# Two transformer layers on one core: every wide product and norm transpose in tiles of 64 rows, values' products in two visits a sample

## The reference

```
mod = silu(c) @ w_mod + b_mod            # shift, scale, gate twice
h = layernorm(x) * (1 + scale) + shift
q, k, v = split(h @ w_qkv + b_qkv)       # 16 heads of 18
# layer 0 only: q and k are layer-normed per head, with a gain
o = softmax(q @ k.T * 18**-0.5) @ v
x = x + gate * (o @ w_proj + b_proj)
h = layernorm(x) * (1 + scale2) + shift2
x = x + gate2 * (gelu(h @ w1 + b1) @ w2 + b2)     # 1152 hidden
```

## Time and profile before

| | |
|---|---|
| time, median of 3 runs | 2496.43 us (2495.59 to 2497.12) |
| profiled execution | 2496.4 us from its first to its last instruction, with nothing outside that span given |
| TensorE matmul busy | 2328.6 us, 93% |
| TensorE weight loads busy | 1975.0 us, 79% |
| VectorE busy | 1899.0 us, 76% |
| ScalarE busy | 1643.7 us, 66% |
| GpSimd busy | 733.8 us, 29% |

### The profile page before, as it was taken

The page is one execution under the profiler, slowest core; times in us unless marked ns, Lnnn a source line. Parts: engine busy times, 40 slices in busy tenths (PEclk is TensorE's granted clock), DMA queues, the critical chain, the costliest instruction groups (busy, mean ns, idle before and its releaser), DMA issues.

```text
span 2496.4 us, 74800 instructions
## 1 busy us (share of the span) xinstructions
PE 2328.6 (93%) x29875; PEld 1975.0 (79%) x29875; DVE 1899.0 (76%) x3456; ACT 1643.7 (66%) x3305; POOL 733.8 (29%) x938
## 2 busy tenths in 40 slices
PE   5658999999999999999899899999999999999988
PEld 3446888888888888888788788888888888888877
DVE  6457888778778888877777788778877887787764
ACT  2356777777777777776666666666666666666653
POOL 2111332333233233323222223233322332233222
PEclk7778999999999999999999999999999999999999
DMA  3777667766765776576666565455555564555431
GB/s 100 143 178 121 113 123 125 123 119 123 130 112 122 127 117 126 122 129 113 131 113 109 133 112 99 100 107 109 103 100 105 104 109 98 108 98 109 90 72 44
DMA packets 259280, 282.07 MB, mean 113 GB/s; under 512 B 25930, under 2 KB 243212, under 8 KB 258936
## 3 DMA queue, kind: packets, MB, share of 16 engines
q1 hardware_dynamic: 243888, 247.40, 53.1%
q10 hardware_dynamic: 15048, 29.89, 5.5%
HBM read 101.86 MB, written 26.73 MB: 52 GB/s over the span
## 4 chain that ended last, share of the span: by engine, by line
PE 66%; DMA 9%; SPq 7%; DVE 6%; issue 4%; POOL 4%; ACT 2%; DVEq 0%; ACTq 0%; POOLq 0%
PE psum L838 17%; PE psum L1082 15%; PE psum L961 8%; PE psum_max L838 6%; SPq L1497 5%; PE psum_exp L937 4%; PE psum L828 4%; PE psum_max L950 4%; DMA attn_k_stack<-attn_qk_hi 4%; PE psum_exp L838 3%; DMA attn_o_and_sums<-attn_o_transposed 3%; DVE attn_maxima L1237 2%; SPq L1447 2%; PE psum_max L866 1%; POOL mlp_ln_split L1439 1%
## 5 line engine op out<-in xcount | busy, mean ns | idle before, releaser
L1237 DVE TENSOR_REDUCE attn_maxima<-psum_max 128x4 f32<-128x1024 f32 x512 | 621.8, 1214 | 202.4 <-PE psum_max L950 201.6
L1102 ACT ACTIVATE attn_probs<-psum_exp 128x1024 f32<-128x1024 f32 x512 | 524.4, 1024 | 166.9 <-PE psum_exp L937 157.7
L1082 PE MATMUL psum<-mlp_w_fc_hi,mlp_hidden_hi 64*128 64x288 f32 (+1 forms) x2250 | 343.6, 293 | 0.5 <-ACT mlp_hidden L1184 0.5
L1082 PE MATMUL psum<-mlp_w_fc_hi,mlp_hidden_lo 64*128 64x288 f32 (+1 forms) x2250 | 343.6, 292 | 0.0
L1082 PE MATMUL psum<-mlp_w_fc_lo,mlp_hidden_hi 64*128 64x288 f32 (+1 forms) x2250 | 341.2, 290 | 0.0
L1410 POOL TENSOR_TENSOR mlp_x<-mlp_x,mlp_gated 128x288 f32<-128x288 f32 x128 | 119.7, 935 | 616.9 <-DVE mlp_gated L1254 616.9
L961 PE MATMUL psum<-attn_probs,attn_v 128*32 128x256 f32 x4096 | 281.5, 393 | 2.1 <-DVE attn_neg_max_lo L1264 1.8
L937 PE MATMUL psum_exp<-attn_q_stack,attn_k_stack 64*128 64x256 f32 x2048 | 245.2, 317 | 21.3 <-DMA attn_q_stack<-attn_neg_max_lo 10.2
L838 PE MATMUL psum_max<-mlp_ln_split,mlp_w_fc_stacked 64*128 64x256 f32 (+1 forms) x3584 | 264.5, 284 | 0.1
L838 PE MATMUL psum<-attn_ln_split,w_qkv_split 128*128 128x256 f32 (+3 forms) x2282 | 251.4, 291 | 12.5 <-ACT attn_qk_squares L1148 5.2
L937 PEld LDWEIGHTS psum_exp<-attn_q_stack,attn_k_stack 64*128 64x128 f32 x2048 | 158.5, 187 | 129.8 <-issue 73.9
(11 more groups left out here) (181 smaller groups left out, 4496.4 us busy)
## 6 DMA issues: line engine op xcount, KB each, us to landing
attn_q_stack<-attn_qk_hi SPq DMA_DIRECT2D x256, 128.0 KB
attn_k_stack<-attn_qk_hi SPq DMA_DIRECT2D x256, 128.0 KB
attn_o_and_sums<-attn_o_transposed SPq DMA_DIRECT2D x256, 128.0 KB, 3.3
mlp_gate_and_gated_bias<-modulation ACTq DMA_DIRECT2D x64, 288.0 KB, 4.9
attn_qk_squares<-qk_rstd SPq DMA_DIRECT2D x32, 512.0 KB
attn_q_stack<-attn_qk_lo SPq DMA_DIRECT2D x128, 128.0 KB
attn_k_stack<-attn_qk_lo SPq DMA_DIRECT2D x128, 128.0 KB
attn_x<-in_x_dram SPq DMA_DIRECT2D x32, 288.0 KB, 6.0
```

What stands on the lines that cost most here:

```text
L1082: mm = q.matmul(to[t], (h_hi, h_hi, h_lo)[kind][r, c, t * P:t * P + P], (w2_hi, w2_lo, w2_hi)[kind][r, c, :], start=(i == 0 and not second ...
L1102: q.activation(probs[r][:], ps_exp[:], ACT.Exp, scale=SCORE_SCALE).then_inc(S["exps"], 1)
L1237: q.tensor_reduce(maxes[g % 2][:, p // QUARTER, :, p % QUARTER, :], ps_max[:].rearrange("p a (t n) -> p a t n", t=TT), AX.X, ALU.max).then ...
```

## The change

- `spaced` goes. q/k, v, projection, fc1 and fc2 are always cut in halves of 64 rows. The last q/k chunk is cut as well: its two token halves are two products of 128 tokens in two banks, in two parts, LAST_FIRST and LAST_SECOND.
- fc1 runs its nine chunks in one loop: the lower rows of one chunk beside the upper rows of the chunk two steps later.
- The norm transposes take 64 tokens each, twelve in place of six, into two banks by token half; ScalarE reads both banks with one instruction.
- The values' products come in two visits a sample, of two groups each, side by side in bank 4 (512 columns), with one copy for both; P_RING goes from 3 to 4.
- The tiles of the modulated norm and of the gated product are shared by attention and MLP, with waits for the other's use.
- The slots are eighths rather than quarters, and nearly all offsets and banks are new. Offsets of TensorE's work are shown, those of the other engines' are left out, as is the bookkeeping of banks and semaphores.

```diff
+VISITS = GROUPS // 2
...
-STACK_RING, V_RING, P_RING, XA_RING, XR_RING = 2, 3, 3, 2, 3
...
-SPAN, STEP = 16, 4
+STACK_RING, V_RING, P_RING, XA_RING, XR_RING = 2, 3, 4, 2, 3
...
+SPAN, STEP = 16, 8
...
-LN_TR, LN_Y, LN_SPLIT = (-46.25, -30.5, {B + 1: -35.25}), (-46.75, -31.25, {B + 1: -35.5}), (-40.25, -30.75)
...
+LN_TR, LN_Y, LN_SPLIT = (-46.625, -31.125, {B + 1: -34.75}), (-47.5, -31.25, {B + 1: -35.125}), (-39.5, -30.25)
...
-LAST_CHUNK_AT = (-34.5, -27.5, {3: -36.0})
-QK_FIRST, QK_SECOND = [(-33.0, -26.0, {B - 1: -31.75}), (-32.75, -16.75)], [(-32.25, -25.0, {B - 1: -31.5}), (-32.25, -16.75, {2: -32.0, B - 1: -31.5})]
...
-V_FIRST, V_SECOND, V_OUT = (-26.0, -17.75, {1: -31.0, B: -17.5}), (-25.5, -17.5, {1: -30.0, 2: -24.0, B + 1: -16.0}), [(-25.0, -17.5, {1: -29.5}), (-24.25, -16.75)]
-VAR_AT, RS_AT = (-28.75, -28.75, {B - 1: -29.0}), (-29.0, -29.0, {0: -31.5})
...
-MAX_AT, MAX_OUT, MAX_TR, NEG_AT, NEG_PLACE = -11.5, -11, [(-4.25, -4.25), (3.75, 5.5, {ALL - 1: 3.0})], [(-4.5, -4.5), (4.25, 5.25)], [(-3.75, -6.0, {0: 0.25}), (5.5, 3.25, {B: 7.0})]
-EXP_AT, EXP_OUT, PV_AT, PV_OUT = 0, 0.25, 5.75, 5.75
...
-XR_AT, GATE_AT, PROJ_FIRST, PROJ_SECOND = (23.75, 21.5, {B - 1: 23.25}), (24.0, 22.5), (26.5, 26.5), (27.0, 28.75)
...
-LAST_FC1_AT, FC1_AT, HIDDEN_AT, H_SPLIT = (49.75, 48.75, {B: 47.75}), 49.75, 49.75, [(49.75, 50.0), (49.75, 50.25), (50.0, 50.25), (50.25, 50.75), (50.5, 50.75)]
+LAST_FIRST, LAST_SECOND = (-34.75, -26.375, {3: -33.75}), (-34.25, -26.25, {3: -33.5})
+QK_FIRST, QK_SECOND = [(-33.625, -25.625, {B - 1: -33.625}), (-32.0, -16.25)], [(-32.75, -24.5, {B - 1: -32.125}), (-31.25, -16.125, {2: -30.625, B - 1: -30.625})]
...
+V_FIRST, V_SECOND, V_OUT = (-27.25, -18.125, {1: -28.625, B: -17.5}), (-26.0, -17.375, {1: -24.75, 2: -23.25, B + 1: -17.625}), [(-25.125, -17.375, {1: -22.875}), (-22.875, -17.0)]
+VAR_AT, RS_AT = (-29.0, -56.625, {B - 1: -28.5}), (-28.5, -34.875, {0: -31.875})
...
+MAX_AT, MAX_OUT, MAX_TR, NEG_AT, NEG_PLACE = -11.5, -11.125, [(-4.25, -4.125), (3.875, 3.75, {ALL - 1: 3.875})], [(-4.0, -3.875), (3.25, 4.125)], [(-0.375, 0.75, {0: 1.125}), (3.125, 4.5, {B: 3.25})]
+EXP_AT, EXP_OUT, PV_AT, PV_OUT = 0, 0.125, 3.75, 3.75
...
+XR_AT, GATE_AT, PROJ_FIRST, PROJ_SECOND = (24.875, 28.0, {B - 1: 20.25}), (21.25, 16.75), (26.0, 28.625), (27.5, 29.75)
...
+TR2, Y2, SPLIT2, SPLIT2_LOW, GATE2_AT = (41.875, 41.125), (41.25, 41.125), (43.625, 43.75, {ALL - 1: 37.25, B: 43.375}), (41.625, 39.0, {ALL - 1: 27.5}), (55.125, 51.5)
+FC1_AT, HIDDEN_AT, H_SPLIT = 49.75, 48.875, [(50.25, 50.0), (50.25, 50.625), (50.25, 50.625), (50.625, 50.625), (50.875, 51.25)]
...
-FC2_AT = [(49.75, 50.0), (51.0, 50.5), (55.75, 55.5), (56.75, 57.25)]
...
+FC2_AT = [(50.125, 50.0), (54.875, 53.25), (56.625, 56.125), (57.625, 57.625)]
...
-TURN_BANKS, LN_REST_BANK, LN2_REST_BANK = ((4, 4), (7, 2)), (3, 7), (7, 7)
-FC1_FIRST, FC1_SECOND, LAST_FC1_BANK = (0, 1, 2, 3), ((5, 4, 0, 1), (6, 4, 0, 1)), (7, 6)
-QK_BANKS, LAST_CHUNK_BANK, VAR_BANK = [((4, 7), (7, 4)), ((5, 6), (6, 5))], (6, 7), 4
-V_BANKS, PROJ_BANKS, FC2_BANKS = ((4, 7), (7, 4)), ((7, 5), (7, 5)), ((5, 6), (5, 6))
-LN_BANK, LN2_BANK = (5, 5), (1, 0)
+TURN_BANKS = ((7, 7), (7, 7))
+FC1_BANKS = ((1, 7, 4, 0, 5, 6, 3, 2, 0), (7, 2, 0, 1, 3, 6, 5, 4, 1))
+QK_BANKS, LAST_CHUNK_BANK, VAR_BANK = [((4, 7), (7, 4)), ((5, 6), (5, 4))], (5, 0), 7
+V_BANKS, PROJ_BANKS, FC2_BANKS = ((4, 7), (7, 6)), ((7, 5), (4, 5)), ((5, 6), (6, 5))
+LN_BANK, LN2_BANK = (2, 5), (0, 2)
...
+FC1_STEPS, FC1_APART = [5, 7, 8, 0, 1, 2, 3, 4, 6], 2
+FC1_BEGUN = [0, 2, 1, 3, 4, 5, 6, 7, 8]
...
+def visit_at(T, off):
+
+    last = VISITS * ALL
+    if T in (LAST_PV, LAST_PV_OUT):
+        return last if (T, off) in ((LAST_PV, PV_AT), (LAST_PV_OUT, PV_OUT)) else None
+    w, r = divmod(T - off, SPAN // VISITS)
+    return int(w) if r == 0 and 0 <= w < last else None
+
+
+def groups_of(w):
+
+    return [s for s in (2 * w - 1, 2 * w) if 0 <= s < GROUPS * ALL]
...
+        y2_ab, y2_c = y_ab, y_c
...
+        gated2 = gated
...
+        LOWER, UPPER = slice(0, HALF_ROWS), slice(HALF_ROWS, P)
...
+        def lower_and_upper(q, low, high, half):
+
+            for i in range(len(WIDE_PAIRS)):
                 done_low = part_matmul(q, low, i, LOWER, i == 0, False)
                 done_high = part_matmul(q, high, i, UPPER, i == 0, False)
...
+            done_low.then_inc(S[half], 1)
+            done_high.then_inc(S[half], 1)
+            halves[half] = halves.get(half, 0) + 2
+
+        def upper_and_lower(q, low, high):
 
             for i in range(len(WIDE_PAIRS)):
-                first, last = not split and i == 0, i == len(WIDE_PAIRS) - 1
-                done_low = part_matmul(q, low, i, UPPER if split else ROWS, first, last)
-                done_high = part_matmul(q, high, i, LOWER if split else ROWS, first, last)
+                last = i == len(WIDE_PAIRS) - 1
+                done_low = part_matmul(q, low, i, UPPER, False, last)
+                done_high = part_matmul(q, high, i, LOWER, False, last)
             return done_low, done_high
...
+        def to_channels(q, banks, src):
+
+            for c in range(3):
+                cols = slice(c * P, c * P + P) if c < 2 else slice(2 * P, XC)
                 for t in range(TT):
-                    mm_ab = q.transpose(ab[:, c * N + t * P:c * N + t * P + P], src[:, t, c * P:c * P + P], ident[:])
-            for t in range(TT):
-                mm_last = q.transpose(last[0:K3, t * P:t * P + P], src[:, t, 2 * P:XC], ident[:])
-            return mm_ab, mm_last
-
-        def ln_modulate(q, g, kind, turned, free, from_banks, to_ab, to_c, done):
+                    for bank, r in zip(banks, (LOWER, UPPER)):
+                        mm = q.transpose(bank[0:cols.stop - cols.start, c * P + t * HALF_ROWS:c * P + t * HALF_ROWS + HALF_ROWS], src[r, t, cols], ident[r, r])
+            return mm
...
+            def last_product(g, t):
+                return (psum[banks["qk", g, 4, t][0]][0:QK_ROWS[4], 0:P], w_attn, slice(4 * P, 4 * P + QK_ROWS[4]), acts, slice(t * P, t * P + P), True, LAST_ROWS)
+
...
+                if (w := visit_at(T, PV_AT)) is not None:
+                    bank = bank_of(("pv", w))
+                    for s in groups_of(w):
+                        g, grp = divmod(s, GROUPS)
+                        if grp == 0:
+                            q.wait_ge(S["v_ready"], TT * (g + 1))
+                        q.wait_ge(S["exps"], PAIRS * g + 2 * grp + 2)
+                        cols = slice(N * (s % 2 == 0), N * (s % 2 == 0) + N)
+                        for t in range(TT):
+                            for i in range(PV_HEADS):
+                                pair = PAIRS * g + 2 * grp + i // HALVES
+                                mm = q.matmul(bank[32 * i:32 * i + VW, cols], v_sb[g % V_RING][:, t, grp * PV_HEADS + i, :, :].rearrange("p r c -> p (r c)"),
+                                              probs[pair % P_RING][:, i % HALVES, t * N:t * N + N], start=(t == 0), stop=(t == TT - 1))
+                        mm.then_inc(S["pv"], 1)
...
+                if (g := due(T, LAST_FIRST)) is not None:
...
+                    bank_of(("qk", g, 4, 0))
+                    bank_of(("qk", g, 4, 1))
+                    lower_and_upper(q, *[last_product(g, t) for t in range(TT)], "last_half")
+                    LAST_HALVES[g] = halves["last_half"]
+                if (g := due(T, LAST_SECOND)) is not None:
+                    q.wait_ge(S["last_half"], LAST_HALVES[g])
+                    low, high = upper_and_lower(q, *[last_product(g, t) for t in range(TT)])
+                    high.then_inc(S["qk_mm"], 1)
...
+                        q.wait_ge(S["qk_half"], QK_HALVES[g, n])
+                        low, high = upper_and_lower(q, *[qk_product(g, c) for c in pair])
...
+                    q.wait_ge(S["v_half"], halves["v_half"])
+                    low, high = upper_and_lower(q, *[v_product(g, t) for t in range(TT)])
...
+                    q.wait_ge(S["proj_half"], halves["proj_half"])
+                    low, high = upper_and_lower(q, *[proj_product(g, t) for t in range(TT)])
...
+                    for k in range(CHUNKS):
+                        low, high = [fc1_product(g, FC1_STEPS[(k + n) % CHUNKS]) for n in (0, FC1_APART)]
+                        low_ends, high_ends = k >= FC1_APART, k + FC1_APART >= CHUNKS
+                        if not low_ends:
+                            bank_of(("fc1", g, FC1_STEPS[k]))
+                        if not high_ends:
+                            bank_of(("fc1", g, FC1_STEPS[k + FC1_APART]))
+                        if low_ends:
+                            q.wait_ge(S["fc1_half"], CHUNKS * g + (2 if k == FC1_APART else k + 1))
+                        for i in range(len(WIDE_PAIRS)):
+                            ends = i == len(WIDE_PAIRS) - 1
+                            done_low = part_matmul(q, low, i, LOWER, i == 0 and not low_ends, ends and low_ends)
```

(16 more changed lines are left out.)

259 lines of the change are left out of this document (101 added, 158 removed).

## The result

The changed kernel takes 2517.59 us (median of four runs, 2515.91 to 2521.16), the kernel before 2496.01 beside it (2494.86 to 2497.12): a ratio of 1.0088, 95% interval [1.0074, 1.0102]. The forecast was 2435, and both the time and its sign are wrong.

What follows compares the result with a forecast made beforehand. TensorE's stream was taken to set the steady pace. Net gains of 0.9 us over 30 layer 0 samples and 1.1 over 31 layer 1 samples sum to 61 us: 2496.4 - 61 = 2435 us, range 2398 to 2475.

Steps and rivals of the forecast that it cites:

- Waits: TensorE's waits for banks and other engines: gain of 0.1 us a sample in layer 0, 0.8 in layer 1 (bounds 0, 1.4).
- the other edits cost nothing here: Shared norm and gate tiles and fourth probabilities buffer: cost 0, covered by VectorE's 200 us idle in each stretch.
- The rival with this mechanism: Waits take the gain as VectorE and ScalarE do the same work in less time: about 2470 us, chance 0.16.
- The prediction's own sign of being wrong: It would be wrong if transposes took 1.3 us or TensorE's list of waits grew past 1 us a sample.
- The rival priced at 2515: Slower: halves' weight loads don't overlap, norm transposes run singly, 1.3 us more a sample; chance 0.05.
- The shared gate tile makes VectorE wait for GpSimd's add: Named a new tight place in the gate products; cost nothing, covered by VectorE's idle time.
- The stacks: In the waits rival (chance 0.16): q/k stacks land in fewer slots before scores; 9 waits, 3.5 us in all, before.
- Switches removed: Fewer changes of TensorE's tile, 0.33 us a stretch: saves 1.8 us a sample in layer 0, 1.5 in layer 1.
- Halves without a visit between: Wide products' second half waiting for its first, with no scores visit as cover: 0.33 us each.
- Last chunk's own tile: Last q/k chunk in 64 x 64 tiles counts as a stretch of its own: 0.33 us a sample (below: 0).
- Transposes: Norm transposes, six becoming twelve of 64 rows in six rounds: no extra cost, upper bound 1.3 us a sample.
- Start, change of layers, tail: Parts outside the steady samples of the two layers: no gain or loss counted.

Runs made afterwards that it cites:

- p1: Kernel before with the MLP's gated tile shared with attention's and GpSimd's additions moved beside their products: 2582.0 us, ratio 1.0340.
- u2: Changed kernel with layer 0's second gate product moved from slot 28.0 to 27.5, ahead of the MLP splits: 2583.5 us, ratio 1.0346.
- u16: Changed kernel with two gated tiles, layer 0's second gate product at 27.5, MLP splits at 46.0, first negated maxima at -4.125: 2504.0 us, ratio 1.0026.
- u10: Changed kernel with layer 0's MLP splits moved from 43.625 to 46.0 and first negated maxima from -4.0 to -4.125: 2523.0 us, ratio 1.0103.
- r1: Changed kernel with VectorE's three MLP split instructions of layer 0 doing only 32 of 256 columns, leaving work out: 2490.3 us, ratio 0.9977.
- u4: Changed kernel with layer 0's MLP split moved from 43.625 to 44.125 and first negated maxima from -4.0 to -4.125: 2534.7 us, ratio 1.0160.
- u14: u10 with layer 0's first norm statistics moved from -65.75 to -62.5: 2538.8 us, ratio 1.0170.
- b2: Kernel before with q/k, v, projection and fc2 always cut in halves of 64 rows, order unchanged: 2532.5 us, ratio 1.0143.
- u6: Changed kernel with layer 0's last chunk in banks 6 and 7, q/k pairs in 4/5 and 7/6, no slot moved: 2541.2 us, ratio 1.0180.

## Why the prediction was wrong, step by step

**The step that failed is "Waits", and the cover behind "the other edits cost nothing here".** It gave layer 0 a gain of 0.1 us a sample; the list of waits grew by 51.8 us in 980, 2.0 us a sample. It gave layer 1 a gain of 0.8; the list grew by 15.4, 0.6 a sample. The 200 us of idle VectorE were an average over whole samples. Where the gate products and the negated maxima fall there was none: in the rows above VectorE works from 844.33 to 847.64 without a gap. The rival with this mechanism was priced at 2470, with layer 0 gaining nothing; it lost 1.0 us a sample. The prediction's own sign of being wrong, waits past 1 us a sample, came true. The rival priced at 2515 has the measured time by luck: its transposes one by one didn't happen.

- *The shared gate tile makes VectorE wait for GpSimd's add*, taken at nothing: 86 us in the kernel before, together with the additions' new slots (p1). In the changed kernel it doesn't show as a wait, since the splits fill the time between the two products. Out of there they gain nothing while the tile is one (u2), and with two tiles u16's order is the best found. How much of the changed kernel's loss is the tile's isn't shown, since against u10 u16 changes layer 0 by only 0.12 us a sample, 0.30 at the full clock, and by two edits at once.
- *VectorE's order.* r1 shows that its load there costs 0.7 us a sample, most of the 1.0 lost, but not the 0.9 that was to be gained; u4, u10 and u14 show that another order moves the wait (last chunk, stacks, head maxima) and hardly shrinks it.
- *The stacks*, named among the rivals with 3.5 us of waits: 26.2 now. In 500 to 1100 us the wait of 14.9 us falls to 0.6 and 2.5 in u4 and u10, where the negated maxima come first, 0.63 us behind their transpose, and TensorE waits for head maxima instead. It stays at 15.5 in r1, where they come 1.16 behind it. What sets it between these is open.
- *The halves alone*, which the prediction's prices made a small gain: 36 us lost in the old order (b2), 0.77 us a sample in layer 0 and 0.45 in layer 1. How much of that is left in the new order no run shows.
- *The clock*, taken as full: some 10 to 12 us in layer 0 and at the change of layers.

**Switches removed, 1.8 and 1.5: each piece as forecast, the sum not confirmed.** Two groups of values take 1.86 us (843.23 to 845.09; forecast 1.88), with scores of 0.34 behind. A sample less its listed waits went from 35.91 to 34.90 us in layer 0 and from 34.66 to 33.64 in layer 1, 1.0 each. With the two terms below at what they measured, layer 0 should give 1.8 - 0.6 + 0.6 = 1.8 and layer 1 1.5 - 0.9 + 0.6 = 1.2; that leaves 0.8 and 0.2 unexplained. The clock is 0.2 of layer 0's. Some may be TensorE's restarts behind waits, which I didn't count (1.60 us from the maxima's scores to the last chunk, of which the scores take 0.23 and 1.21 are marked). The rest is open.

**Halves without a visit between, 0.33: right.** In layer 1 the projection's two halves take 2.30 us from start to start:

```profile
1925.99 2.46 PE L856 MATMUL psum<-w_proj_split,attn_o_split 64*128 64x288 f32 x28
1928.29 1.09 PE L856 MATMUL psum<-w_qkv_split,attn_ln_split 64*128 64x288 f32 x14
```

14 rounds of 0.131 are 1.83; of the 0.46 over, some 0.1 is the restart of the first half, and the rest, 0.33 or a little more, the second's.

**Last chunk's own tile, 0.33: mis-sized, it is 0.** 847.24 to 848.41 is 1.17 us: 14 rounds of 0.06 are 0.84, the uncovered half is 0.33, and nothing is left.

**Transposes, 0: mis-sized the other way.** Twelve of the MLP norm take 0.33 us with their exit (839.69 to 840.02), where I had 0.65: 0.3 less, twice a sample.

**Start, change of layers, tail, nothing: wrong at the change.** It costs 14 us. FC1 waits there (1180 to 1480 us) for the head maxima 12.6 us in 11 times, which the kernel before doesn't, and the clock is at 1.2 GHz for 13.6 us more. No run took that apart; it stays open, as does what holds layer 1 at 35.2.

## What to carry to other kernels

When TensorE is the bound and a change takes some of its work away, look at each other engine's order in the slots where TensorE will arrive earlier, not at its idle share over the whole. A tile shared by two producers on one engine and freed by another ties two in-order queues together; look for the longest thing in the freeing queue, even where the trace of the tuned result shows no wait for it. When you move an instruction out of the way of one wait, check who holds the next bank or tile that it takes (u6) and who stands behind it (u4, u14): none of the eleven kernels here that only moved slots or banks of the changed one was faster than that one. And compare the granted clock before you give a longer sample to a wait.

## What the runs showed of the hardware

A tile of 64 x 64 runs among tiles of 64 x 128 without the 0.33 us that a stretch of 128 x 32 costs: the last chunk's 1.17 us above are its rounds and the uncovered half. Transposes of 64 rows overlap in pairs. Twelve lie in 0.52 us (839.69), the last one 0.22 long by its mean, so five rounds take 0.30, some 0.06 each:

```profile
L856 PE MATMUL psum<-attn_ln_split,w_qkv_split 64*64 64x128 f32 x832 | 41.6, 233 | 32.5 <-issue 27.5 <-DVE attn_ln_split L1382 3.0
...
L885 PE MATMUL psum_exp<-identity,mlp_ln_normed 64*128 64x64 f32 x256 | 13.9, 221 | 0.0
```

VectorE's split of the norm's rest takes 0.48 us alone and 1.42 beside GpSimd's low part (u10, VectorE, then GpSimd):

```profile
773.29 1.42 DVE L1394 SCALAR_TENSOR_TENSOR mlp_ln_split<-ln_rest_hi,minus_one_on_low_rows,attn_ln_modulated_rest 96x256 fp32r<-96x256 f32 x1
...
773.13 1.29 POOL L1477 TENSOR_TENSOR mlp_ln_split<-attn_ln_modulated,mlp_ln_split 128x512 fp32r<-128x512 f32 x1 [1.61 <-DVE mlp_ln_split L1387]
```

The Trainium skill has the rule for it: a VectorE operation with two inputs in SBUF and a GpSimd operation that reads SBUF exclude each other for the whole instruction (SBUF — State Buffer, SBUF: two separate sides). The trace agrees: 1.42 is about the 1.13 that were left of GpSimd's 1.29 and part of its own 0.48. In the changed kernel the cast just before it is the longer one, 0.88 us beside GpSimd's addition where it took 0.28 in the kernel before, and the split then takes 0.83 (rows of VectorE above). The three splits together are no longer than before, 2.1 us.
